# Four layers on eight images: projection and layer 3 behind the loop, softplus polynomial in PSUM

## The reference, cut to what matters

```python
x = x + L0(gn(x))   # 1x1 and 2x2 convolutions, four state-space scans, gate, projection
x = x + L1(gn(x))   # attention, 8 heads, 1024 x 1024
x = x + L2(gn(x))   # deformable convolution: 16 groups x 9 sampled points of 4 corners, then out @ out_w
x = x + L3(gn(x))   # x * p, p by 20 power iterations of a 1024 x 1024 matrix

delta = softplus(einsum('blr,dr->bld', dts, dtw) + dtb)        # inside L0
samp = (v00*(1-wx) + v01*wx)*(1-wy) + (v10*(1-wx) + v11*wx)*wy # inside L2, summed over 9 points with a mask
```

## Time and profile before

| | us |
|---|---|
| three runs | 14502.23, 14509.67, 14512.0 (median 14509.67) |
| profiled execution | 14510.48 |
| its span, first to last instruction | 14508.8 |
| mean granted TensorE clock | 0.774 of full speed |
| busy: TensorE matmuls, VectorE, GpSimd, ScalarE | 8229.5, 10025.0, 9729.9, 2946.7 |

### The profile page before, as it was taken

One profiled execution on the slowest core, in us unless ns is written; L12 is line 12 of the kernel. 1 busy time (PEld: TensorE's weight loads), 2 busy tenths in 40 slices (PEclk: granted clock), 3 DMA queues, 4 the chain that ended last, 5 costly groups with the idle time before them and its releaser, 6 DMA issues. The chain is left out here.

```text
span 14508.8 us, 98770 instructions
## 1 busy us (share of the span) xinstructions
PE 8229.5 (57%) x32544; PEld 4053.4 (28%) x32544; DVE 10025.0 (69%) x9864; ACT 2946.7 (20%) x4731; POOL 9729.9 (67%) x9221
## 2 busy tenths in 40 slices
PE   5780567555576467565586566665575566760005
PEld 3240324223242323322242223323242232420002
DVE  6753796669776797759866697758876697753333
ACT  2230213112231213212131212212231122300000
POOL 0006767777677767777677767777677776777771
PEclk8895679787798678886798778887797778985558
DMA  1012111421122211321123211321114211322111
GB/s 69 9 30 66 50 43 58 105 72 48 54 72 83 72 45 57 93 86 48 53 62 94 72 47 56 88 90 50 44 58 104 72 49 54 80 76 59 54 54 45
DMA packets 890429, 913.09 MB, mean 63 GB/s; under 512 B 692418, under 2 KB 702658, under 8 KB 880643
## 3 DMA queue, kind: packets, MB, share of 16 engines
q0 software_dynamic: 294912, 604.57, 14.7%
q1 hardware_dynamic: 594946, 301.65, 7.2%
HBM read 770.26 MB, written 135.28 MB: 62 GB/s over the span
## 5 line engine op out<-in xcount | busy, mean ns | idle before, releaser
L121 POOL DMA_INDIRECT gat<-corner_tables,idx x9216 | 9729.4, 1056 | 4491.5 <-issue 2726.6
L135 DVE TENSOR_TENSOR gat<-gat,wts 128x1152 f32<-128x1152 f32 x1024 | 1385.7, 1353 | 1480.5 <-DMA gat<-corner_tables,idx 1352.6
L139 DVE TENSOR_REDUCE dcn<-gat 128x32 f32<-128x1152 f32 x1024 | 2153.1, 2103 | 38.7
L756 PE MATMUL PS<-hc,ident 128*128 128x512 f32 (+2 forms) x4096 | 1931.2, 630 | 234.8 <-DVE hc L796 197.7
L819 DVE TENSOR_TENSOR_SCAN hs<-dA,PS 128x1024 f32<-128x1024 f32 x672 | 1533.0, 2281 | 51.8 <-ACT dA L773 21.6
L756 PEld LDWEIGHTS PS<-hc,ident 128*128 128x128 f32 x4096 | 1001.3, 277 | 839.5 <-issue 459.4
L796 DVE TENSOR_TENSOR hc<-hs,PS 128x1024 f32<-128x1024 f32 x672 | 802.8, 1195 | 0.8 <-issue 0.8
L1028 PE MATMUL PS<-ident,E 128*128 128x128 f32 x4096 | 579.0, 287 | 348.0 <-ACT ET L1097 194.9
L1107 ACT ACTIVATE E<-PS,nmax 128x1024 f32<-128x1024 f32 x512 | 569.9, 1113 | 840.7 <-DVE nmax L1162 650.4
L735 PE MATMUL PS<-bc1b,pick 96*128 96x512 bf16 x1024 | 400.1, 499 | 596.3 <-DVE hc L796 596.1
L1162 DVE TENSOR_REDUCE nmax<-PS 128x1 f32<-128x1024 f32 x512 | 601.9, 1217 | 190.9 <-PE PS L1017 190.9
(11 more groups left out here) (247 smaller groups left out, 11482.9 us busy)
## 6 DMA issues: line engine op xcount, KB each, us to landing
gat<-corner_tables,idx POOLq DMA_INDIRECT x9216
corner_tables<-xp SPq DMA_DIRECT2D x1024, 64.0 KB, 2.2
D<-in_dist_dram SPq DMA_DIRECT2D x8, 4096.0 KB, 14.2
wqkv<-in_qkv_w_dram SPq DMA_DIRECT2D x8, 3072.0 KB, 11.7
corner_tables<-gat SPq DMA_DIRECT2D x1, 17280.0 KB, 54.5
X<-in_x_dram SPq DMA_DIRECT2D x32, 512.0 KB, 5.4
w_in<-in_in_w_dram SPq DMA_DIRECT2D x16, 1024.0 KB, 7.0
w_c<-in_c_w_dram SPq DMA_DIRECT2D x16, 1024.0 KB
```

Of the source, the lines that this page charges most:

```text
L121: nc.gpsimd.indirect_dma_start(bd.gat[n % NG][:, k * 4 * CG:(k + 1) * 4 * CG], None, bd.rows, bass.IndirectOffsetOnAxis(ap=bd.idx[:, m, g ...
L135: nc.vector.tensor_tensor(v, v, wv, ALU.mult).then_inc(self.prod, 1)
L139: nc.vector.tensor_reduce(bd.dcn[m % 2][:, g * CG:(g + 1) * CG], gat[:].rearrange("p (k c) -> p c k", c=CG), AX.X, ALU.add).then_inc(self. ...
L756: mm = nc.tensor.matmul(PS[:, p.ybank(d, h), 0:p.hl], self.ident[:], src[:, j, h * p.hl:(h + 1) * p.hl], start=(c == 0 and j == 0), stop=( ...
```

## The change

The loop does layers 0 and 1 and the preparation only; a `Gather` knows its image and stores its sampled values in a tensor for all images. Behind the loop `rest(b)` does projection and layer 3, for images 0 to 6 with the gather of image 7 spread over them. `SHARE` is written anew. In `l0_steps`, `q` lies in the PSUM banks of the argument, and TensorE's wait before it fills them becomes one for L697 of the pass before.

```diff
@@ Gather.keep
-            sp.dma_start(self.bd.io["dcn"][m * P:(m + 1) * P, :], self.bd.dcn[m % 2][:])\
+            dst = self.bd.io["sampled"][bass.ds(self.image, 1)].rearrange("a n c -> (a n) c")
+            sp.dma_start(dst[m * P:(m + 1) * P, :], self.bd.dcn[m % 2][:])\
@@ l0_steps
                         if i:
-                            pe.wait_ge(sp_in, 3 * (DT * (i - 1) + t) + 2)
+                            pe.wait_ge(sp_out, DT * (i - 1) + t + 1)
...
-                    q = [qb[t][:, 0:p.L] for t in range(DT)]
+                    q = [PS[:, 4 + 2 * t:6 + 2 * t, :].rearrange("p a f -> p (a f)")[:, 0:p.L] for t in range(DT)]
@@ l2_prepare_in (everything under "if finish" goes, but for this)
-        if finish:
+        if self.bg:
             self.gather_only(PT * G)
             self.bg.close()
-        self.bg = Gather(self)
+        self.bg = Gather(self, b)
@@ l2_output
-                    sp.dma_start(dc[:], io["dcn"].rearrange("(m p) f -> p m f", p=P)).then_inc(d_loaded, 16)
+                    sp.dma_start(dc[:], io["sampled"][bass.ds(b, 1)].rearrange("a (m p) f -> p (a m) f", p=P))\
+                        .then_inc(d_loaded, 16)
                     sp.dma_start(w_out[:], io["out_w2"][:]).then_inc(w_loaded, 16)
                     sp.dma_start(X[:], io["keep"][bass.ds(b, 1)].rearrange("a p t f -> p (a t) f"))\
                         .then_inc(x_back, 16)
+                self.background(block, SHARE["project"], first=loads)
...
+                    spread = Spread(self, dve, 1)
+                    spread()
                     dve.wait_ge(x_back, 16)
@@ shares and order
-SHARE = {"finish": 4, "norm3": 1, "gram": 7, "power": 12, "norm0": 2, "conv": 5, "steps": 8, "scan": 38, "norms": 5,
-         "out": 2, "norm1": 1, "attention": 28, "norm2": 1, "prepare": 13}
+SHARE = {"finish": 1, "norm0": 2, "conv": 6, "steps": 9, "scan": 46, "norms": 6, "out": 2, "norm1": 2, "attention": 34,
+         "norm2": 1, "prepare": 18, "project": 2, "norm3": 1, "gram": 5, "power": 10}
+def image(bd, b):
+    if bd.bg:
+        bd.bg.image = b - 1
+    bd.layer0(b, first=not bd.bg)
+    bd.end_stage()
+    bd.layer1()
+    bd.end_stage()
+    bd.l2_prepare(b)
+    bd.end_stage()
+def rest(bd, b):
+    if b == BATCHES - 1:
+        bd.gather_only(PT * G)
+        bd.bg.close()
+        bd.bg = None
+    bd.l2_output(b)
+    bd.end_stage()
+    bd.layer3(b)
+    bd.end_stage()
@@ program
+        image(bd, 0)
+        with nc.Fori(1, BATCHES) as b:
+            image(bd, b)
+        bd.bg.image = BATCHES - 1
+        for b in range(BATCHES):
+            rest(bd, b)
```

More of the change, by code:

```diff
@@ L95, with __init__ @@
     NG = 5
-    def __init__(self, bd):
-        self.bd, nc = bd, bd.nc
+    def __init__(self, bd, image):
+        self.bd, self.image, nc = bd, image, bd.nc
         self.sems = bd.gather_sems
@@ L472, in layer0 @@
                 hc = [self.sb(c2, f"hc{i}", [P, N]) for i in range(2)]
-                with ExitStack() as c3:
-                    q = [self.sb(c3, f"q{i}", [P, N]) for i in range(DT)]
-                    self.l0_steps(passes, xw, dtw, (hs, hc), (dA[0:2], dA[2:4]), q)
+                self.l0_steps(passes, xw, dtw, (hs, hc), (dA[0:2], dA[2:4]))
                 self.l0_recurrence(passes, dA, hs, hc)
@@ L590, in _, with l0_steps @@
                 act.wait_ge(conv_out, len(groups))
-    def l0_steps(self, passes, xw, dtw, ebufs, rbufs, qb):
+    def l0_steps(self, passes, xw, dtw, ebufs, rbufs):
         nc, PS = self.nc, self.PS
@@ L1263, in store @@
             def store(sp):
-                if not finish:
-                    sp.wait_ge(self.table_zero, 16 * 2)
+                sp.wait_ge(self.table_zero, 16 * 2)
                 for m in range(PT):
@@ L1459, in _ @@
                 o.step(nc.vector.tensor_tensor(wts[:, :, 2], low, wts[:, :, 3], ALU.subtract))
[L1460 to L1466, removed]
-                self.bg.rest(dve)
[L1468 to L1499, removed]
-                                             PS[:, 4 + m % 4, :].rearrange("p (k f) -> p k f", k=CT), ACT.Copy)\
-                            .then_inc(d_out, 1)
+                self.bg.rest(dve)
     def l2_output(self, b):
@@ L1512, in l2_output, with loads @@
             with Stage(nc) as block:
-                @block.sync
-                def _(sp):
-                    sp.dma_start(dc[:], io["dcn"].rearrange("(m p) f -> p m f", p=P)).then_inc(d_loaded, 16)
+                def loads(sp):
+                    sp.dma_start(dc[:], io["sampled"][bass.ds(b, 1)].rearrange("a (m p) f -> p (a m) f", p=P))\
+                        .then_inc(d_loaded, 16)
                     sp.dma_start(w_out[:], io["out_w2"][:]).then_inc(w_loaded, 16)
@@ L1527, in _ @@
                                                        in1=x, op0=ALU.add, op1=ALU.add).then_inc(p_added, 1)
+                    spread.end()
+                    dve.wait_ge(p_added, 2 * CT)
                 @block.tensor
@@ L1767, in store @@
         sp.wait_ge(stored, 16 * CT)
-SHARE = {"finish": 4, "norm3": 1, "gram": 7, "power": 12, "norm0": 2, "conv": 5, "steps": 8, "scan": 38, "norms": 5,
-         "out": 2, "norm1": 1, "attention": 28, "norm2": 1, "prepare": 13}
+SHARE = {"finish": 1, "norm0": 2, "conv": 6, "steps": 9, "scan": 46, "norms": 6, "out": 2, "norm1": 2, "attention": 34,
+         "norm2": 1, "prepare": 18, "project": 2, "norm3": 1, "gram": 5, "power": 10}
 BATCHES = NB
 SLOTS = 2
-def image(bd, b, head, tail):
-    if head:
-        bd.layer0(b, first=not tail)
-        bd.end_stage()
-        bd.layer1()
-        bd.end_stage()
-        bd.l2_prepare(b, finish=tail)
-        bd.end_stage()
-    else:
+def image(bd, b):
[9 more added lines that the diff above has]
+    if b == BATCHES - 1:
         bd.gather_only(PT * G)
@@ L1792, in image @@
         bd.bg = None
-        bd.l2_output(b - 1)
-        bd.end_stage()
-    if tail:
-        bd.layer3(b - 1)
-        bd.end_stage()
-    else:
-        bd.gather_only(SHARE["norm3"] + SHARE["gram"] + SHARE["power"])
+    bd.l2_output(b)
+    bd.end_stage()
+    bd.layer3(b)
+    bd.end_stage()
 def program(nc, io):
@@ L1805, in program @@
     rows = TW * TW * G
-    io = dict(io, tables=nc.dram_tensor("corner_tables", (SLOTS, rows, 4 * CG), F32, kind="Internal").ap())
+    io = dict(io, tables=nc.dram_tensor("corner_tables", (SLOTS, rows, 4 * CG), F32, kind="Internal").ap(),
+              sampled=nc.dram_tensor("sampled", (NB, N, C), F32, kind="Internal").ap())
     with ctx:
@@ L1811, in program @@
         bd.end_stage()
-        image(bd, 0, True, False)
-        if BATCHES > 1:
-            with nc.Fori(1, BATCHES) as b:
-                image(bd, b, True, True)
-        image(bd, BATCHES, False, True)
+        image(bd, 0)
[4 more added lines that the diff above has]
+            rest(bd, b)
 def _tiles(a, t):
```

15 lines of the change are left out of this document (3 added, 12 removed).

## The result

| | before | changed |
|---|---|---|
| median, us | 14510.83 | 14276.89 (14261.9 to 14284.5, four runs) |
| ratio, 95% interval | | 0.9839 (0.9822 to 0.9856) |
| profiled span | 14508.8 | 14260.3 |

The forecast was 14249.

What follows compares the result with a forecast made beforehand. The gather on GpSimd was taken as the floor, VectorE nearly balanced with it. Image 0 1142.6 + 13, seven iterations 10794, then 25 + 1995 + 278: 14248 us of span, 14249 as time; range 14080 to 14500 for 8 in 10.

Steps and rivals of the forecast that it cites:

- T: One loop iteration from index cast to index cast: 1542 us instead of 1662.5, bound by the gather.
- waits for sums in it: GpSimd's waits for VectorE's sums (L139) in an iteration: 68.5 us go, 3 left.
- held time in it: GpSimd's DMA time above 0.944 us each in an iteration: 146 us before, changed by -55 in sum.
- polynomial: Softplus steps (L688) in `l0_steps`: running value in PSUM takes 19 us off held time, bounds 0 and 24.
- attention: Attention stage: held time falls 15 us as VectorE waits for data, bounds 0 and -18.
- image 0: Softplus path up to image 0's cast: +13 us, of it 9 waits, large steps +2, four large L683 +2.
- a rest beside the gather: After the last cast, one projection and layer 3 beside image 7's gather: 285 us (278 to 295).
- after the last cast: Behind the loop: 25 us for weights and one unit, 1995 for seven rests, 278 for the end.
- the rival of the waits: Loop: VectorE behind in the scan, the 68.5 us of waits for sums stay; time 14900 or 14704, chance 0.14.
- held per product everywhere: Loop: moved units keep 0.6 us held each, -27 instead of -55; T = 1570, time 14445, chance 0.15.
- VectorE's wait for data: Iteration: VectorE waits 110 us for gathered data; sign: over 80 us, in attention and preparation above all.
- a stretch of 63.6 us without a matmul: Sign for the whole kernel: no stretch without matmuls longer than some 30 us.

Runs made afterwards that it cites:

- order_again: Changed kernel with the polynomial's running value back in SBUF and TensorE's old wait, so only the image order is new: 14349.63 us, 0.9895 of the kernel before.
- mix2b: Changed kernel with two images' projection and layer 3 back in iterations 6 and 7, units spread by another table: 17188.7 us, kernel before beside it 17434.22, ratio 0.9861.

## Why the prediction was right

| step | predicted | measured |
|---|---|---|
| T | 1542 | 1547.2 |
| waits for sums in it | 3 | 1.8 |
| held time in it | 91 | 99 |
| of it: polynomial | -19 | -18 |
| attention | -15 | -8 |
| preparation | -6 | -5 |
| scan | +4 | +3 |
| layer 3 leaves | -22 | -21 |
| image 0 | +13 | +11.2 |
| a rest beside the gather | 285 | 282.6 |
| after the last cast | 2298 | 2276 |

*The reading of the bound held.* The price of an iteration was taken as GpSimd's own list (DMAs, pauses, held time), and the sum closes to 0.1 us. The scan gave the gather 436 DMAs, 48.4 units for 46 summed, as argued (+2), so the rival of the waits found nothing to wait for; such waits came back only at the level where TensorE is slow beside the gather. That the span came within 12 us of the forecast is in part luck: the loop took 36 us more than forecast (7 x 5.2), the tail 22 less and image 0 2 less.

*The held time was seen where it is made.* The polynomial went as predicted. Attention did not: 293.44 - 296 x 0.944 = 14 us remain where 6.6 were forecast. I had priced its products as in the bare gather, 0.09 us each; they hold less than before but not that little: in the timeline about 11 of the 14 us lie under them, some 3 under attention's own instructions that read SBUF alone (L1156, L1187). Held time is 8 us above the forecast in all, 7 of them here, and the 3 us left for waits didn't come (the 1.8 are six pauses of 0.3): T's 5. Attention's held time is the mis-sized term. The rival "held per product everywhere" (T = 1570) fails by more: 14 us in attention for 34 units against 21.6 for 29.

*PSUM's price was mostly the waits.* In the first large pass of image 0 VectorE waits 3.34 + 2.19 us for ScalarE. The first two lines are of the kernel before, the others of the changed one:

```profile
125.44 0.69 DVE L683 TENSOR_SCALAR q<-hs 128x1024 f32<-128x1024 f32 x1
127.06 0.70 DVE L683 TENSOR_SCALAR q<-hs 128x1024 f32<-128x1024 f32 x1 [0.93 <-ACT hs L659]
...
128.72 1.23 DVE L683 TENSOR_SCALAR PS<-hs 128x1024 f32<-128x1024 f32 x1 [3.34 <-ACT hs L659]
132.14 1.23 DVE L683 TENSOR_SCALAR PS<-hs 128x1024 f32<-128x1024 f32 x1 [2.19 <-ACT hs L659]
133.27 18.19 DVE L688 SCALAR_TENSOR_TENSOR PS<-PS,hs 128x1024 f32<-128x1024 f32 x16
```

It had waited 0.93 us there, and 0 in the second large pass, where it now waits 5.5: the two passes have 10 us of new waits, where 7 were forecast. The operand costs something too: L683 takes 1.23 us instead of 0.69, 2 us over the four large ones, as forecast. The sixteen steps take 18.19 us with a PSUM operand and 18.25 without, so the +2 for them was wrong. The Trainium skill ("VectorE: DVE Perf Modes", TRN2 errata) gives a fixed 120 cycles from PSUM and 58 from SBUF for results written to SBUF, and would have made the steps longer; the steps here write PSUM too, and these rows show no difference.

*Held by two SBUF operands.* The Trainium skill's "SBUF — State Buffer", section "Who interferes with whom", names two SBUF inputs as contending with GpSimd's reads but infers that descriptor generation isn't stalled by `tensor_tensor`. The pair of order_again and changed decides for the polynomial's instruction: 1.97 us a DMA with both operands in SBUF, 0.94 with one in PSUM; for a `tensor_tensor` it is the 2.98 us of the earlier trace rows. The held DMA also takes its row numbers from `idx` in SBUF. Whether that read or the descriptors are held no run separates, so the rows agree with the first statement and leave the inference open.

*One term and one sign were off.* VectorE's wait for data is 204.1 us where the prediction counted on 110 and named over 80 as the sign. Part of it covers what VectorE would have waited for anyway: in the convolution stage, for one, it waits 37.4 us for data while TensorE is busy 47.35 of 58.9 us. And a stretch of 63.6 us without a matmul does exist, in the preparation before every cast; one of 47.6 us was there before, so it says nothing against the forecast.

## What to carry to other kernels

Write the iteration as the list of each engine, pauses included, and see which list closes to the iteration's length; work moved off that iteration is worth what shortens that list, less what it costs where it lands. An engine that only issues DMAs can be slowed by what another engine reads: one PSUM operand in a long VectorE chain gave back 14 us an iteration. When background work is moved, level the waits on both sides: here a mixture of both orders beats either.

## What was not expected of the hardware

In nine runs TensorE was slow in stages beside the gather, while image 0, which has no gather beside it, takes 1141 to 1160 us in all nine. Image 0 and the convolution stage of mix2b, then the same stage of the changed kernel:

```profile
0.00:1155.60 1155.60, 789.96 (x2966) 397.12 (x2966) 733.62 (x761) 338.67 (x552) 0.46 (x5) 0.84 0.12 35
...
4997.00:5140.50 143.50, 67.69 (x145) 30.01 (x146) 20.69 (x12) 10.67 (x17) 82.65 (x87) 0.62 0.14 40
```

```profile
4306.20:4365.10 58.90, 47.35 (x144) 25.32 (x145) 20.96 (x12) 11.10 (x17) 44.58 (x48) 0.91 0.17 53
```

Image 0 takes the usual 1155.6 us. Beside the gather the matmuls of the convolution need 143.5 us for 58.9. Two records of TensorE's timeline in mix2b, and one of the changed kernel, where twenty go in 8.75 us:

```profile
5040.14 1.01 PE L570 MATMUL PS<-XN,w_in 128*128 128x512 f32 x1 [1.79 <-issue]
5043.64 1.01 PE L570 MATMUL PS<-XN,w_in 128*128 128x512 f32 x1 [2.49 <-issue]
```

```profile
4319.63 8.75 PE L570 MATMUL PS<-XN,w_in 128*128 128x512 f32 x20
```

The starts in mix2b are 2.1, 2.8 or 3.5 us apart, with idle time that the profile puts down to issue. The stage isn't slow from its start. Three windows of it in mix2b:

```profile
5007.00:5017.00 10.00, 10.00 (x24) 4.37 (x23) 2.23 (x2) 0.00 (x0) 7.56 (x9) 1.00 0.18 52
5047.00:5067.00 20.00, 7.02 (x7) 2.01 (x7) 3.44 (x2) 1.97 (x2) 15.12 (x17) 0.50 0.19 52
5107.00:5117.00 10.00, 1.01 (x1) 0.00 (x0) 0.00 (x0) 0.00 (x0) 0.00 (x0) 0.50 0.00 0
```

In the first, TensorE works without a pause beside nine DMAs of the gather; in the second it starts seven matmuls in 20 us beside the same traffic. In the third GpSimd has stopped. TensorE starts the last matmul of this group at 5107.34, ScalarE takes up its result only at 5121.35, and from 5125.86 TensorE goes on at its usual pace. So the gather's traffic isn't enough to make it slow, and a pause of 14 us falls where no DMA of the gather runs. The clock doesn't start it either: matmuls of 0.59 us start at 5021.22 and 5024.01, 2.8 us apart, before the records get as long as 1.01 us. The granted clock is 1.00 in the first window and 0.50, the level of 1.2 GHz, in the second. One chip gave both levels of time at different times, with the same kernel before. What slows the issue isn't known.
